# A wait on SyncE: the loads behind the second pack are issued once x^T of group 0 has landed

## What is computed

```python
def ada_rms(x, t, w, tw):
    n = x * rsqrt(mean(x ** 2, axis=-1) + 1e-6)
    return n * (w * (1.0 + t @ tw.T))[:, None, :]

h = ada_rms(x, time_emb, ln1_w, ln1_tw)
q, k, v = h @ Wq.T, h @ Wk.T, h @ Wv.T      # 8 query heads of 32, one key/value head
q, k = apply_rope(q, pos), apply_rope(k, pos)
attn = softmax(q @ k.T / sqrt(32))          # within a sequence of 32 tokens
x = x + (attn @ v) @ Wo.T
h = ada_rms(x, time_emb, ln2_w, ln2_tw)
out = x + silu(h @ Wg.T) * (h @ Wu.T) @ Wd.T   # inner width 1024
```

## Time and profile before

| | us |
|---|---|
| median of 3 runs | 115.08 (114.5 to 116.61) |
| the profiled execution itself | 114.3 |
| its span, from the first to the last instruction | 112.5 |
| busy: PE / PEld / DVE / ACT / POOL | 105.2 / 97.7 / 65.8 / 52.7 / 62.5 |

### The profile page before, as it was taken

The page is one execution under the profiler, slowest core; times in us unless marked ns, Lnnn a source line. Parts: engine busy times, 40 slices in busy tenths (PEclk is TensorE's granted clock), DMA queues, the critical chain, the costliest instruction groups (busy, mean ns, idle before and its releaser), DMA issues.

```text
span 112.5 us, 2416 instructions
## 1 busy us (share of the span) xinstructions
PE 105.2 (93%) x776; PEld 97.7 (87%) x776; DVE 65.8 (59%) x172; ACT 52.7 (47%) x141; POOL 62.5 (56%) x92
## 2 busy tenths in 40 slices
PE   5949888999999999699999999999999999999990
PEld 4837666768999998698999999999999999999990
DVE  0329995789985762507876543579485352855311
ACT  5057968639358465203492255146531731444300
POOL 1006459568599999984569994234522520455600
DMA  3999999500000000000020000000200000200011
GB/s 75 151 367 409 301 370 419 214 3 0 0 0 3 6 0 0 0 0 3 6 93 0 0 0 6 0 3 0 99 0 0 0 3 6 93 0 0 0 51 48
DMA packets 3708, 7.68 MB, mean 68 GB/s; under 512 B 624, under 2 KB 1648, under 8 KB 3696
## 3 DMA queue, kind: packets, MB, share of 16 engines
q1 hardware_dynamic: 3552, 7.51, 19.7%
q10 hardware_dynamic: 144, 0.01, 0.1%
HBM read 6.47 MB, written 1.05 MB: 67 GB/s over the span
## 4 chain that ended last, share of the span: by engine, by line
PE 62%; POOL 12%; DVE 10%; issue 7%; DMA 5%; ACT 2%; SPq 1%; DVEq 0%; POOLq 0%; ACTq 0%
PE ps_gu L417 30%; DMA xt<-in_xT 5%; POOL hf_l L1094 4%; PE ps_d L265 3%; PE ps_a L266 3%; PE ps_a L267 3%; PE ps_d L266 3%; PE ps_a L265 3%; PE ps_d L267 3%; PE ps_a L370 2%; PE ps_s L382 2%; POOL wgu_l L1102 2%; DVE rot_b L625 2%; PE ps_s L343 2%; DVE ps_a L638 2%
## 5 line engine op out<-in xcount | busy, mean ns | idle before, releaser
L1094 POOL TENSOR_TENSOR hf_l<-hf,hf_h 128x256 fp32r<-128x256 f32 x32 | 23.6, 737 | 24.9 <-ACT hf_h L972 24.9
L417 PE MATMUL ps_gu<-h_h,wgu_h 128*128 128x256 f32 x120 | 25.2, 292 | 0.0
L965 ACT ACTIVATE th<-ps_gu 128x256 f32<-128x256 f32 x32 | 12.2, 382 | 26.3 <-PE ps_gu L417 25.7
L417 PE MATMUL ps_gu<-h_h,wgu_l 128*128 128x256 f32 x120 | 23.9, 281 | 0.0
L417 PE MATMUL ps_gu<-h_l,wgu_h 128*128 128x256 f32 x120 | 23.9, 280 | 0.0
L764 DVE SCALAR_TENSOR_TENSOR sg<-th,ps_gu 128x256 f32<-128x256 f32 x32 | 13.2, 414 | 16.5 <-ACT th L965 16.4
L417 PEld LDWEIGHTS ps_gu<-h_h,wgu_h 128*128 128x128 f32 x120 | 18.6, 189 | 0.2
L417 PEld LDWEIGHTS ps_gu<-h_h,wgu_l 128*128 128x128 f32 x120 | 18.4, 189 | 0.0
L417 PEld LDWEIGHTS ps_gu<-h_l,wgu_h 128*128 128x128 f32 x120 | 18.4, 188 | 0.0
L972 ACT ACTIVATE hf_h<-hf 128x256 fp32r<-128x256 f32 x32 | 13.2, 411 | 9.5 <-DVE hf L773 9.5
L773 DVE TENSOR_TENSOR hf<-sg,ps_gu 128x256 f32<-128x256 f32 x32 | 13.4, 420 | 1.0
(11 more groups left out here) (136 smaller groups left out, 203.0 us busy)
## 6 DMA issues: line engine op xcount, KB each, us to landing
wgu<-in_w_gu SPq DMA_DIRECT2D x4, 512.0 KB, 9.1
xt<-in_xT SPq DMA_DIRECT2D x4, 256.0 KB, 7.0
wd<-in_w_d SPq DMA_DIRECT2D x2, 512.0 KB, 12.3
out_x<-xk SPq DMA_DIRECT2D x3, 256.0 KB, 2.2
pb<-in_pack_b SPq DMA_DIRECT2D x1, 576.0 KB, 6.7
xk<-in_x_tok SPq DMA_DIRECT2D x2, 256.0 KB, 8.3
xk<-in_x_tok SPq DMA_DIRECT2D x1, 512.0 KB, 11.2
wqkv<-in_w_qkv SPq DMA_DIRECT2D x1, 320.0 KB, 5.8
```

The lines of the kernel that those rows point to most:

```text
L417: mm = pe.matmul(ps_gu[:, slot % RING, part, cols], w[:, m, span(part * KH + k, 1, P)], h[:, k, cols], start=(step == 0 and k == 0), stop= ...
L965: act.activation(th[:, n % RING], ps_gu[:, n % RING, 0, :], ACT.Tanh, scale=0.5).then_inc(th_ready, 1)
L1094: pool.tensor_tensor(hf_l[:, m], hf[:, m], hf_h[:, m].bitcast(F32), ALU.subtract).then_inc(hf_lo, 1)
```

## The change

SyncE waits for the semaphore of xt of group 0 behind the issue of pb (pack_b) and ahead of the issue of xt of group 2. All issues behind it keep their order.

```diff
             sp.dma_start(xt[:, 0], xT[:, 0]).then_inc(in_xt[0], 16)
             sp.dma_start(wqkv[:, :, :], w_qkv).then_inc(in_wqkv, 16)
             sp.dma_start(pb[:, :], pack_b).then_inc(in_pb, 16)
+            sp.wait_ge(in_xt[0], 16)
             sp.dma_start(xt[:, 2], xT[:, 2]).then_inc(in_xt[2], 16)
             sp.dma_start(xt[:, 3], xT[:, 3]).then_inc(in_xt[3], 16)
             sp.dma_start(wgu[:, 0:2, :], w_gu[:, 0:2]).then_inc(in_wgu[0], 16)
```

## The result

The changed kernel takes 117.93 us (median of 4 runs, 117.29 to 118.32) where the kernel before took 114.81 us beside it: a ratio of 1.0253, 95% interval [1.0203, 1.0302]. It is slower. The profiled execution took 117.98 us, its span is 116.2 us.

A forecast was written before the change was run, and what follows sets the result against it. Mostly TensorE work bounds the kernel, with x^T's load at the start. Landing 0, held loads 0.1 us hidden behind 0.3 us of slack, wait under 0.1 us on a non-urgent queue: 115.1 us, range 113.6 to 116.8.

The forecast's parts named there:

- The landing of x^T: Load of x^T of group 0 at the kernel's start: still lands near 6.86 us, gain taken as 0.
- The byte count: Bytes issued against bytes moved: no held load had moved a byte when x^T landed at 6.86 us.
- The first rival: Issuing the held loads slows x^T's load; x^T lands 1.4 to 1.9 us earlier, 113.8 us; chance 0.22, partial effect included.
- The queue stays fed: Behind the wait SyncE issues a load per 0.47 us, and a 256 KB load takes 0.66 us to move.
- D: Delay of all held loads' landings caused by the wait: 0 to 0.15 us, taken as 0.1.
- The hole by bytes: Gap in the DMA stream near 8.0 us, before the first held byte moves: 0 to 0.15 us.
- The slack of 0.3 us: Lateness of held loads that ScalarE can spare around the second exponential before the end moves: 0.3 us.
- the way by which D reaches the end: Through ScalarE's copy of wgu chunk 2 ahead of the exponentials; beyond 0.3 us the end moves one for one.
- The third rival: The stream restarts slowly at 8 us: held loads 2.05 us late, second exponential 1.5 us later, 116.6 us; chance 0.16.
- The first rival's note: Lighter HBM load might shorten the 1.3 us from last byte to landing; only 72 to 154 GB/s moved before x^T's landing.

The follow-up runs named there:

- e16: The changed kernel with ScalarE's copy of wgu chunk 2 behind group 0's exponentials and both turned-probability copies, plus four warming matmuls: ratio 1.0025 to the kernel before.
- e6: The kernel before with four warming matmuls in place of one ahead of the mean square: ratio 0.9994 to the kernel before.
- e5: The changed kernel run once more, unaltered: ratio 1.0192 to the kernel before.
- e2: The changed kernel with the wait in its place but on pos instead of x^T of group 0: ratio 0.9996 to the kernel before.
- e3: The kernel before with the wait on x^T of group 0 three issues further down, ahead of xk of group 0: ratio 1.005.
- e8: The kernel before with x^T laid out by group in HBM, so each of its loads reads one piece: ratio 0.9934.
- e11: The changed kernel with x^T, x by token, wgu and wd all laid out by load in HBM: ratio 0.9898 to the kernel before.
- e9: The changed kernel with only x^T laid out by group in HBM: ratio 0.9979 to the kernel before.
- e14: The changed kernel with the wait one issue earlier, ahead of pb, so pb is held too: ratio 1.0318 to the kernel before.
- e7: The changed kernel with four warming matmuls in place of one ahead of the mean square: ratio 1.0187 to the kernel before.

## Why the prediction was wrong

The forecast was 115.1 us in 113.6 to 116.8; measured were 117.9.

- **The landing of x^T: right.** The byte count said that the held loads take nothing from it; it landed at 6.85 us instead of 6.86. The first rival is out for this wait.
- **"The queue stays fed", D = 0 to 0.15 us: the step that failed.** The hole by bytes was rightly small, but D measured 2.4 us (wgu chunk 2 at 17.8 against 15.4). I took the time from one issue to its first byte and the landing of pa as the cost of a start. Both are from the first load of a stream, and the first load is not slow: in the kernel before the third one, xt of group 0, took 5.2 us, and rates of 72 and 154 GB/s stood beside it. The row for what a restart costs was there, and I used it only for the rival. What the runs showed in its place: 178 to 338 GB/s from 7 to 12 us where 387 to 422 were moved before, and a landing 2.4 us later.
- **The slack of 0.3 us and the way by which D reaches the end: right.** e16 shows that ScalarE's copy of wgu chunk 2 carries the cost. The size fits too: 2.4 us less 0.3 is the 2.1 us on the chain, and in e6, where the copy started 0.49 us later than in the kernel before (15.95 us), the copy of the turned probabilities started 0.17 us later (17.42).
- **The third rival: the mechanism that happened, undersized.** It had 770 thousand bytes missing and D = 2.05 us, against 712 (from 7 to 12 us) and 2.4 measured. It did not see that the slow stretch would be spread over five us, nor that a second dip would be deeper: at 13 to 15 us 231 and 209 GB/s were moved, where the kernel before has one dip, of 199, at 12 to 13 us and 332 and 352 behind it. It had 1.5 us on the chain against 2.1. And it had no term for the clock: TensorE idles 2.0 to 2.6 us in front of the turned probabilities, and where the clock fell behind that (e5), 1.3 us came on top. 2.1 and some 1 us make the 3.1 between the medians. I gave the case 0.16.
- **Against it** I had argued that wqkv and pb still flow when the held loads are issued. They did, and it was not enough: 376 thousand bytes were left when SyncE came back; with 1014 and 1385 (e2, e3) the ratio stayed at 1.0 and 1.005.
- **A reading that does not hold.** The first rival's note sets 72 to 154 GB/s beside the landing of x^T. Those are the rates from 4 to 6 us; in the us that ends with the landing 385 GB/s were moved, and the 1.3 us between last byte and landing were pb's, at over 400. The rows say nothing there on a lightly loaded HBM. No number of the forecast hangs on it.
- **The page that spoke against the change.** The Trainium skill (DMA: Bandwidth & Descriptors, Rules for kernel authors) says to issue early and wait late. The runs agree on the direction: 1.019 to 1.025 for the wait, 1.032 for the wait one load earlier. The page speaks of a fixed setup cost; here the cost was a lower rate for some 5 us.

Not settled: why a stream is slow from about one to four us behind its start. Rows 8 KB apart make it worse (e8 against the kernel before: x^T at 5.4 and 6.9 us, ratio 0.9934), but e11 has no such rows and still a slow stretch; in e9 it meets wgu, in the changed kernel x^T. Nor was it tried whether the many small rows of pos and small have a part in the slow start of the kernel. No run took the two apart at the packets of one DMA engine. The Trainium skill (DMA: Bandwidth & Descriptors, Latency and other measured facts) has a case of rows far apart that halve the rate, at distances of 4 MiB; no run here has such distances, and none has tried others than 8 KB, the 16 KB of wgu and one piece.

## What to carry to other kernels

Before you hold loads back, count what will still be queued when they are issued. When a queue drains and starts again, look up in the trace what its first start cost, over all of its first us and not for the first load alone, and take that as the price. A late load costs by the instruction that waits for it, and by what stands behind that instruction on an in-order engine: move a copy that is needed much later behind the ones that are needed now, all of them, before touching the loads. And lay inputs out in HBM by load: here that gave 1.0%.

## What was not expected of the hardware

- In 128 rows of 2 KB at 8 KB from each other x^T of group 0 landed at 6.5 to 7.6 us in twelve profiles and at 5.8 in one (e14, pb held); in one piece it landed at 5.1 to 6.3 us in six.
- The rate behind a restart fell to 178 GB/s in the first profile of the changed kernel, and to 193 GB/s (share 0.57) where every load was one piece.
- The granted clock fell to 0.50 behind waits of TensorE of 2.0 (e14), 2.2, 2.3, 2.6 and 2.7 us, and stayed at 1.00 behind waits of 2.0 (e7) and 2.3 us (the changed kernel).
